# Four chained conditioned blocks on one core: the transposes of the scores wait once for both halves

## The reference

```python
scores = jnp.einsum('bhqd,bhkd->bhqk', q / math.sqrt(HEAD_DIM), k)
scores = scores + attention_bias          # (32, 16, 256, 256)
scores = jnp.where(src_mask, -jnp.inf, scores.astype(jnp.float32))
probs = jax.nn.softmax(scores, axis=-1).astype(v.dtype)
ctx = jnp.einsum('bhqk,bhkd->bhqd', probs, v)
...
x = x + (ctx @ Wo + bo)
h = _ln(x) * g2 + beta2
ff = _gelu2(h @ W1 + b1) @ W2 + b2
return x + ff
```

## Time and profile before

| | |
|---|---|
| median of three executions | 2071.33 us (2069.99 to 2072.31) |
| the profiled execution | 2071.33 us, its span 2069.5 us |
| busy share: TensorE matmul, weight load | 93%, 81% |
| busy share: VectorE, ScalarE, GpSimd | 77%, 67%, 12% |
| TensorE idle before the transposes of L687 | 61.4 us for the matmuls, 147.2 us for the weight loads |
| a batch of the middle stretch, from head 0's turn to the next | 59.4 us (two matrices), 64.1 us (deep) |

### The profile page before, as it was taken

One profiled execution on the slowest core, in us unless ns is written; L12 is line 12 of the kernel. 1 busy time (PEld: TensorE's weight loads), 2 busy tenths in 40 slices (PEclk: granted clock), 3 DMA queues, 4 the chain that ended last, 5 costly groups with the idle time before them and its releaser, 6 DMA issues.

```text
span 2069.5 us, 43614 instructions
## 1 busy us (share of the span) xinstructions
PE 1921.3 (93%) x14354; PEld 1676.1 (81%) x14354; DVE 1590.7 (77%) x5373; ACT 1376.7 (67%) x2210; POOL 252.4 (12%) x361
## 2 busy tenths in 40 slices
PE   5789999999999999999999999999999999999786
PEld 4668888888888888888888888888888888788676
DVE  4577877787887788887777888778888877877774
ACT  3376677677667677767767767766776776666443
POOL 1111111011111011111001111101111110111100
PEclk9799999999999999999999999999999999999998
DMA  6655555665565566654555655556665546653450
GB/s 221 202 172 167 187 153 158 186 203 182 183 178 148 156 202 192 196 181 154 154 187 183 195 172 179 164 174 201 189 196 181 177 146 177 216 159 118 133 153 11
DMA packets 222311, 356.12 MB, mean 172 GB/s; under 512 B 29523, under 2 KB 120147, under 8 KB 222068
## 3 DMA queue, kind: packets, MB, share of 16 engines
q1 hardware_dynamic: 222068, 352.99, 56.0%
HBM read 294.12 MB, written 58.79 MB: 171 GB/s over the span
## 4 chain that ended last, share of the span: by engine, by line
PE 76%; DVE 12%; issue 5%; ACT 4%; DMA 1%; ACTq 0%; SPq 0%; POOL 0%; DVEq 0%; POOLq 0%
PE pD L471 51%; PE pX L687 11%; PE pS L471 9%; DVE bias_ring L1178 4%; PE pC L471 3%; DVE bias_ring L975 3%; PE pC L709 1%; DVE x_nat L972 1%; ACT L777 1%; DVE crossed L972 1%; ACT gelu_out L777 1%; ACT probs L777 1%; ACT hid L777 1%; DVE res L978 0%; DVE y_nat L978 0%
## 5 line engine op out<-in xcount | busy, mean ns | idle before, releaser
L1178 DVE CUSTOM_DVE_ANT_0 bias_ring<-pS,bias_ring 128x256 f32<-128x256 f32 x1024 | 389.5, 418 | 200.3 <-PE pS L471 197.4
L777 ACT ACTIVATE probs<-pX 128x512 f32<-128x512 f32 x512 | 304.6, 595 | 225.1 <-PE pX L687 222.8
L777 ACT ACT_TABLE_LOAD x341 | 437.5, 1283 | 18.9 <-PE pD L471 12.0
L687 PE MATMUL pX<-ident,bias_ring 128*128 128x128 f32 x2048 | 321.2, 280 | 61.4 <-DVE bias_ring L975 49.3
L687 PEld LDWEIGHTS pX<-ident,bias_ring 128*128 128x128 f32 x2048 | 228.9, 141 | 147.2 <-issue 95.9
L975 DVE TENSOR_SCALAR bias_ring<-bias_ring,row_max 128x256 f32<-128x256 f32 x1024 | 321.8, 357 | 18.3
L471 PE MATMUL pS<-k_stack,q_stack 96*128 96x256 f32 x1024 | 304.5, 379 | 0.0
L471 PE MATMUL pD<-x,raw 128*128 128x256 f32 x1024 | 246.4, 384 | 3.0 <-ACT gelu_out L777 1.0
L471 PE MATMUL pD<-raw,gelu_out 128*128 128x256 f32 x1024 | 237.6, 379 | 0.0
L471 PEld LDWEIGHTS pS<-k_stack,q_stack 96*128 96x128 f32 x1024 | 197.9, 193 | 19.8
L471 PEld LDWEIGHTS pD<-x,raw 128*128 128x128 f32 x1024 | 188.2, 191 | 31.8 <-issue 9.7
(11 more groups left out here) (148 smaller groups left out, 3663.4 us busy)
## 6 DMA issues: line engine op xcount, KB each, us to landing
bias_ring<-in_fside SPq DMA_DIRECT2D x512, 256.0 KB, 4.4
raw<-in_experts SPq DMA_DIRECT2D x128, 512.0 KB, 4.7
q_spill<-hid SPq DMA_DIRECT2D x96, 256.0 KB, 3.4
k_spill<-hid SPq DMA_DIRECT2D x96, 256.0 KB, 3.4
q_stack<-q_spill SPq DMA_DIRECT2D x128, 192.0 KB, 4.3
k_stack<-k_spill SPq DMA_DIRECT2D x64, 384.0 KB, 5.6
norm<-in_expert_rows SPq DMA_DIRECT2D x32, 384.0 KB, 4.1
x_nat<-in_x SPq DMA_DIRECT2D x32, 256.0 KB, 3.1
```

The lines of the kernel that those rows point to most:

```text
L687: last = e.transpose(pX[:, k, t * P:(t + 1) * P], bias_ring[:, u % NBIAS, t, k * P:(k + 1) * P], ident[:, :])
L777: return e.activation(o, i, func, bias=bias, scale=scale)
L1178: e.tensor_tensor_reduce(bias_ring[:, n, t, :], pS[:, t, :], bias_ring[:, n, t, :], 1.0, -3.4e38, ALU.add, ALU.max, row_max[:, n, t:t + 1] ...
```

## The change

VectorE signals `subtracted` once for each head, at the second half, and no longer once for each half. TensorE waits for it once, at the beginning of the turn and ahead of the wait for the exponential, and no longer before each half's two transposes. The instructions that compute stay as they were, and so does their order on each engine.

```diff
                 def turn(h):
                     u = u0 + h
+                    e.wait_ge(sem["subtracted"], u + 1)
                     if u:
                         e.wait_ge(sem["exp_made"], u)
                     for t in range(T):
-                        e.wait_ge(sem["subtracted"], T * u + t + 1)
                         for k in range(K):
                             last = e.transpose(pX[:, k, t * P:(t + 1) * P], bias_ring[:, u % NBIAS, t, k * P:(k + 1) * P], ident[:, :])
                     last.then_inc(sem["turned"], 1)
@@
                     e.wait_ge(sem["max_made"], 2 * u + 2)
                     for t in range(T):
-                        ts(bias_ring[:, n, t, :], bias_ring[:, n, t, :], row_max[:, n, t:t + 1], ALU.subtract).then_inc(sem["subtracted"], 1)
+                        last = ts(bias_ring[:, n, t, :], bias_ring[:, n, t, :], row_max[:, n, t:t + 1], ALU.subtract)
+                    last.then_inc(sem["subtracted"], 1)
```

## The result

The changed kernel takes 2104.43 us (median of four, 2102.9 to 2105.12) against 2071.82 for the one before (also four executions): a ratio of 1.0156, 95% interval 1.0145 to 1.0169, or 32.3 us more. 2101 was forecast, with a range of 2085 to 2116.

The account below looks back on a forecast made before the run. TensorE was taken to bound the kernel (busy 93%), so its idle time counts. Middle batches 25.5 us plus outer batches 4.2 make 29.7 on 2071.33: 2101 us, +1.4%, range 2085 to 2116.

Parts of the forecast that it names:

- the 182 turns: Turns of the scores on TensorE whose first weight load comes 115 to 120 ns after the first subtraction's end.
- Increments at nothing: One increment fewer per head on VectorE was costed at nothing; at most a gain of 3.6 us.
- A satisfied wait costs nothing: Removing the wait in the middle of the turn, where already satisfied, was put at gain 0.
- 0.20 a bound turn: In turns started by the first subtraction, waiting for both halves makes the next scores start at 705 ns, against 505.
- The walk of one batch: Following the delays head by head through one middle batch gave 0.98 us a batch, times 26 = 25.5 us.
- the outer six batches: First three and last three batches: 42 bound turns, 8.4 us at 0.20, half let through: 4.2.
- Order unchanged: Rival: at the turn, the subtraction's wait remains the separate, slower event; +37.5 us, 2109; chance 13%.
- Slack taking half: Rival: VectorE or ScalarE stretches late anyway absorb delays, or some batches give nothing; 2084 to 2090; chance 14%.
- hidden: Rival: four of five stalls vanish and the time stays within 0.2%, less than 4.1 us; chance 4%.
- faster: Rival: the middle wait holds back the sequencer in all 512 turns, so dropping it gains; 2045; chance 3%.
- The increments' 0.02 us: Rival: increments cost VectorE 0.02 us in each bound turn, which comes back; 2097; chance 4%.
- more than summed: Rival: turns now just free become bound, or lags of both engines add; 2115 and over; chance 7%.

## Why the prediction was right

*What bounds.* Right: the 182 turns start on the first half's subtraction, though the view of waits hardly names it. The 85 in the prediction are stalls of matmuls, beside 135 of weight loads; before the loads the subtraction is named for 1.6 us. In the changed kernel, whose subtraction wait rides on the load, the same view names VectorE for 286 stalls of the loads and "issue" for 7. Two counts of the prediction were off. The five bound heads are bound in 25 of the 26 middle batches and not in all, 124 turns and not 130; the total of 140 holds. And 59 turns start some 51 ns after an exponential, not 47: in the other 12, mostly head 12's, the second half comes later still, so that the changed kernel binds them to the subtraction.

*Increments at nothing.* Right (both increments back: no change). The rule of the Trainium skill that I had weighed, some 26 ns for an increment saved (TensorE: Matmul & The Clock Gate, The cost: per-tile semaphore tail), shows no effect on VectorE: the median pair takes 616 ns with one increment and with two. No run here tests it for TensorE's tiles.

*A satisfied wait costs nothing.* Right in the turns of the middle batches that TensorE reaches late: by the records their lag against the kernel before neither grew nor shrank by more than 0.02 from head 1 to head 7 of the batch shown. And in the 230 turns of each trace that load over 0.2 us after the second half, the four loads take 461 ns (median) with the middle wait and without.

*0.20 a bound turn, by 53 instead of 115 ns.* Right, and the order of waits is shown by its own experiment: 8 us, 7 to 8 expected.

*The walk of one batch.* The records of the batch shown give the lags behind head 11's turn of the batch before: 0.20, 0.40, 0.60, 0.46, 0.66, 0.86 us for heads 13, 14, 15, 0, 1 and 8. The walk had these very numbers. The disputed one was head 9, whose 0.16 I put in by half: it vanishes in 20 of the 26 middle batches, the one shown among them, and in four 0.12 to 0.14 of it stays. A batch of the middle stretch grows by 0.96 us on average (0.91 median), 24.9 us over 26 batches, against 0.98 and 25.5. That the mean comes so near is partly luck: head 9 gives 0.04 and not 0.08, and a few irregular batches, two of them 1.4 us longer, lift the mean.

*The term that was mis-sized* is the outer six batches. I let half of 8.4 us through, 4.2. In the changed kernel the stretch from the very first turn to batch 3's first is 2.3 us longer than before, and the one from batch 29's first turn to the end is 4.4 us longer: 6.7 together. The kernel with both increments back, whose waits are the same, has 0.4 and 4.9 there, 5.3 together. So more than half of their lag gets through, and two traces differ by over 1 us in it. Why more gets through I did not isolate; these batches hold turns that were just free and became bound, but that this is the reason is argued, not shown. With 24.9 in the middle the change comes to 31.6 us in the trace; the timed executions have 32.3 (30.0 to 35.0). The profiled spans differ by 34.2, because the changed kernel's first turn starts 2.6 us later (89.42 against 86.78). That stretch the change does not touch, and over all traces here it varies from 86.1 to 91.7.

*The rivals.* Order unchanged (2109): excluded for this kernel by the event's line, and its size confirmed. Slack taking half, hidden, and faster: none happened; faster fails by the free turns. The increments' 0.02 us is excluded by the kernel with both of them back. Of the last rival (more than summed) the condition came true, for 56 turns became bound to the second half, most of them heads 9 and 12, but their lag was mostly absorbed and the time stayed under 2115.

## What to carry to other kernels

In this kernel a wait in the middle of a group of instructions was free where it was met and worth most of one step of the producer (0.20 of 0.27 us) where it was not; count the groups that start at the first producer's end before you merge waits. The lag added up over a loop in which two engines take turns, and was lost where the next stall hung on a chain that had branched off before it; walking one period of the trace stall by stall gave the lag of six heads to 0.01 us, and left only head 9's open. And when a loop of two engines shows up in that walk, look for a member that needn't be in it: here the turn stood between one head's maxima and the next head's scores for no reason of data.

## What the runs showed of the hardware

- With two waits ahead of a weight load, the one first in the program released it 51 to 53 ns after the producer's end, the second one (an event of its own) 113 to 115 ns after. The same holds whichever semaphore is first.
- Where the subtraction's wait rides on the load, the profile names VectorE for the stall (286 stalls, 7 at "issue"); where it is the event, it doesn't (1.6 us with that name before, 135 stalls at "issue").
- Two neighbouring subtractions of 352 ns overlap by 85 ns (medians), with or without an increment on the first.
